# Edge router: GpSimd waits for four indirect fetches before it issues the next four

## The reference, cut to what matters

```python
h = (x_flat @ W_gat).reshape(M, HEADS, NUM_EXPERTS)          # 4 heads, 4 experts
e = leaky_relu(a_src[src] + a_dst[dst], 0.2)                 # per edge and head
ee = exp(e - e_max[dst])
denom = segment_sum(ee, dst)
msg = h[src] * (ee / denom[dst])[:, :, None]
agg = segment_sum(msg, dst) + b_gat
scores = layernorm(agg).mean over heads                      # gates the experts: top 2, softmax
```

## Time and profile before

| what | value |
|---|---|
| median of 3 timed executions | 3129.7 us (3127.84 to 3139.87) |
| span of the profiled execution | 3331.1 us |
| mean granted TensorE clock in it | 0.841 |
| edge router's loop, first fetch to the next stage's first DVE instruction | 2147.66 to 2442.31 us |
| busy shares of the span | PE 76%, DVE 63%, ACT 39%, POOL 22% |

### The profile page before, as it was taken

How to read it: one execution, slowest core, us unless ns; L and a number is a source line. 1 busy time by engine, 2 the same in 40 slices (tenths; PEclk the granted TensorE clock), 3 DMA queues, 4 the chain that set the end, 5 groups by cost and what they waited for, 6 DMA issues and landing times. The chain is left out here.

```text
span 3331.1 us, 50319 instructions
## 1 busy us (share of the span) xinstructions
PE 2524.9 (76%) x18840; PEld 1620.7 (49%) x18840; DVE 2094.1 (63%) x4114; ACT 1309.8 (39%) x2407; POOL 721.2 (22%) x756
## 2 busy tenths in 40 slices
PE   6477999999999999965566178587649989971542
PEld 5334555555555555545255167344326666641542
DVE  6737787778788878856646397654743547761212
ACT  4333444444444444424555004232224444451431
POOL 0000000000000000010064630166610033306244
PEclk7688999999999999987689557698879978885766
DMA  4431112222221121113223101000012221111333
GB/s 76 130 107 42 49 49 49 55 60 53 50 49 49 49 49 49 46 40 121 67 77 75 43 17 18 13 5 5 5 32 70 52 50 41 41 33 56 94 87 93
DMA packets 189058, 178.78 MB, mean 54 GB/s; under 512 B 83700, under 2 KB 162177, under 8 KB 185977
## 3 DMA queue, kind: packets, MB, share of 16 engines
q1 hardware_dynamic: 168064, 137.00, 16.5%
q0 software_dynamic: 20768, 38.75, 4.8%
HBM read 139.11 MB, written 43.64 MB: 55 GB/s over the span
## 5 line engine op out<-in xcount | busy, mean ns | idle before, releaser
L3557 PE MATMUL hy_ps<-hy_uT,hy_win 128*128 128x512 f32 x1152 | 499.3, 594 | 0.0
L3557 PEld LDWEIGHTS hy_ps<-hy_uT,hy_win 128*128 128x128 f32 x1152 | 217.9, 190 | 283.0 <-issue 272.2
L2469 POOL DMA_DIRECT2D ek_w<-ek_src x32 | 17.8, 556 | 1162.6 <-DVE ek_dst L2491 1162.6
L3619 PE MATMUL hy_ps<-hy_wo,hy_yg 128*128 128x512 f32 x512 | 239.6, 613 | 14.5 <-ACT XNP L3762 8.7
L3055 PE MATMUL er_c<-XNG 128*128 128x400 f32 x480 | 184.0, 540 | 0.0
L3619 PEld LDWEIGHTS hy_ps<-hy_wo,hy_yg 128*128 128x128 f32 x512 | 94.2, 193 | 125.6 <-issue 99.3
L2690 PE MATMUL f_px<-XNG 128*128 128x40 bf16 x736 | 69.0, 266 | 98.2 <-DVE XNG L2605 66.0
L3841 DVE TENSOR_TENSOR_SCAN XNG<-XNG,hy_fx 128x2048 f32<-128x2048 f32 x32 | 141.6, 4425 | 3.0 <-issue 0.4
L2988 POOL DMA_INDIRECT er_gone<-er_nodes,er_sidx x120 | 123.7, 1031 | 36.6 <-issue 36.3
L3055 PEld LDWEIGHTS er_c<-XNG 128*128 128x128 f32 x480 | 97.6, 209 | 69.5 <-issue 14.5
L946 DVE TENSOR_TENSOR f_hg<-f_hs,f_gb 128x640 f32<-128x640 f32 x64 | 52.7, 825 | 109.9 <-ACT f_hs L928 91.3
(11 more groups left out here) (698 smaller groups left out, 6123.4 us busy)
## 6 DMA issues: line engine op xcount, KB each, us to landing
XNG<-hy_decays SPq DMA_DIRECT2D x32, 1024.0 KB
hy_rb<-hy_inverse SPq DMA_DIRECT2D x128, 128.0 KB, 3.5
f_gb<-gate_rows SPq DMA_DIRECT2D x16, 640.0 KB, 5.1
g_KB<-g_keys SPq DMA_DIRECT2D x32, 320.0 KB
f_xg<-f_rows SPq DMA_DIRECT2D x54, 128.0 KB
f_ys<-f_ysl SPq DMA_DIRECT2D x54, 128.0 KB
f_y<-f_ysl SPq DMA_DIRECT2D x47, 128.0 KB
f_rows<-in_x_dram POOLq DMA_DIRECT2D x2, 2560.0 KB, 16.0
```

The source lines that it names most:

```text
L3557: mm = pe.matmul(p[:], win[:, t, m * 128:(m + 1) * 128], uT[:, t, :], start=(t == 0), stop=(t == KT - 1))
L3619: mm = pe.matmul(PS[4 + q % 2][:], yg[:, t, q * 128:(q + 1) * 128], wo[:, t, :], start=(t == 0), stop=(t == KT - 1))
```

## The change

In front of the first and of the fifth fetch of `sources`, and in front of `ends`, POOL waits for four semaphores. The values are such that the last four fetches issued have landed. A `sem_inc` on `settled`, which nobody waits for, stands behind each set of waits, as one already did behind the waits for `weighted` and `sought`. Buffers, fetches and their order stay the same.

```diff
-                def sources(par):
+                def sources(par, before):
                     for u in range(GRP):
+                        if u % PARTS == 0:
+                            for i in range(PARTS):
+                                pool.wait_ge(rows_in[par][i], before + (16 if u == 0 else 32))
+                            pool.sem_inc(settled, 1)
                         pool.indirect_dma_start(out=gone[:, par, u, :], out_offset=None, in_=tab_dram,
...
                     pool.wait_ge(weighted, r + 1)
                     pool.wait_ge(sought, r + 2)
                     pool.sem_inc(settled, 1)
+                    for i in range(PARTS):
+                        pool.wait_ge(rows_in[par][i], 24 * (r - par) + 48)
+                    pool.sem_inc(settled, 1)
                     ends(1 - par)
-                    sources(1 - par)
+                    sources(1 - par, 24 * (r + par))
...
                 ends(0)
-                sources(0)
+                sources(0, 0)
```

## The result

The changed kernel takes 3207.4 us (median of 4 executions, 3202.4 to 3218.3); the kernel before took 3134.8 us beside it on the same chip (median of 4). The ratio is **1.0256, 95% interval 1.0222 to 1.0291**: 2.6% slower, some 80 us (0.0256 x 3130). One execution of the unchanged kernel, beside `lagged` and `one_wait`, took 5077.1 us and is in no ratio. The prediction was 3188 us, with 3140 to 3222.

What follows compares the result with a forecast made beforehand. POOL's fetch issue was taken to bound the router; 36 sets at 2.0 us plus the last turns gave +75 us, or +42 with 33 regained. The middle, +58 on 3129.7, gave 3188 us, range 3140 to 3222.

Steps and rivals of the forecast that it cites:

- The bound: Fixed loop of the router: POOL issues a fetch every 1.26 us and bounds 32.1 of a pass's 37.7 us.
- A set costs 2.0 us: At each set on POOL: landing 1.56 plus restart 0.81 less the ordinary gap 0.30, taken as 2.0 us, bounds 1.2 to 2.6.
- the estimate from it: Set of waits priced by the skill page's fixed cost: 1.55 us each, sum +24 to +57, 3170 us in the middle.
- How many sets lie on the path: Sets up to turn 11's first fetches: 2 + 33 + 1 = 36, so 72 us if POOL has no idle time.
- What can be given back: POOL's pauses let PE's count through, so its idle time before `sought` vanishes: 33.4 us back, leaving +42 us.
- the six idle stretches: POOL waiting some 5.9 us for `sought` before every second turn, 1 to 11; 33.4 us in all beyond ordinary gaps.
- the middle between +42 and +75: +58 us, between all profiled idle time being in timed executions (+42) and none (+75); 3188 us, chance 0.60 for 3168 to 3208.
- The last turns: Turns 11, 12 and 13: sets partly covered by DVE's search and PE's end, adding 0.2, 1.9 and 1.4 us.
- The signs announced: New trace: 2.3 us pauses between fours, 44 us passes, `sought` waits gone to turn 11, router end about 2484 us.
- Stretches that stay with the waits on top: Rival: POOL's idle time before `sought` remains and the sets add to it; +64, 3193 us, chance 0.10.
- Dear waits of 2.6 us each: Rival: each set on POOL costs 2.6 us and no idle time is regained; +101, 3231 us, chance 0.10.
- Cheap waits and faster: Rivals: sets at 1.2 us, 3140 us, or no effect, 3130 us, together 0.12; at 0.4 us, 3111 us, chance 0.08.

Runs made afterwards that it cites:

- lagged: The kernel before plus three sets a turn, each one wait for the four fetches before the last four; 3120.7 us, ratio 0.9981.
- one_wait: The changed kernel with one wait in each set instead of four, for the last of the four fetches; 3205.3 us, ratio 1.026 to the kernel before.
- half_sources: The kernel before with only four of the eight source fetches a turn, the other rows zero; 3091.9 us, ratio 0.9893.
- the two gathers: The kernel before with five or six of eight targets gathered by TensorE, not four, so 11 or 10 fetches a turn; ratios 0.9958 and 0.9906.
- again: The kernel before, without an edit, profiled once more; 3123.0 us, ratio 1.0001, profile span 3116.7 us.
- late_sets: The kernel before with the change's sets of waits in the last two turns alone, six sets; 3143.0 us, ratio 1.0037.

## Why the prediction was right in kind and some 20 us low

**The bound: right.** POOL's fetches set the turn. `half_sources` and the two gathers show it: a fetch less makes a turn 1.1 to 1.4 us shorter, until about 12 us.

**A set costs 2.0 us: right.** The pause was expected at 2.1 to 2.5 us and is 2.17 to 2.44 up to turn 10, less 0.30 about 2.0. That it comes from asking for a fetch that hasn't landed is shown from two sides: wait for fetches that have landed and keep the sets, nothing is lost (`lagged`); take three of four waits away and keep the last fetch, nearly all stays (`one_wait`). The two parts of the sum, 1.56 us to the landing and 0.81 us to the restart, are some 1.45 and 0.9 us by the medians of the changed kernel; no run has one without the other. The Trainium skill's rule to issue a DMA early and to wait for it late ("DMA: Bandwidth & Descriptors", section "Rules for kernel authors") agrees with both runs. Its fixed cost of about 2.0 us in "Anatomy of one DMA" is below what these fetches show, 2.2 us at the least and 2.4 in the median, and the estimate from it, 3170 us, was further off.

**How many sets lie on the path: right.** The 36 sets up to turn 11's fetches were put at 72 us; between the two traces they are 69.7 us (group starts at 265.4 and 195.7 us after the first fetch). That POOL already waited 2.21 us for `sought` in one of these turns of `again` accounts for 1.9 us of the difference.

**What can be given back: wrong, and this is the step that failed.** Under "What can be given back" the six idle stretches of 33.4 us were said to vanish, and the forecast went to the middle between +42 and +75. They did vanish, but in the kernel before five of them vanish as well, and the sixth shrinks to 2.21 us (`again`). They belonged to one profiled execution, whose span was 201 us above the timed median. Next to nothing was regained, and the end of the range worked out for this case, +75, was the right one; measured were 78.9 us in the traces and some 80 in the times. The middle of +42 and +75 is 17 us below that end for this reason alone, most of the 21 us that the forecast of +58 lacks. The result stayed inside the range because the range had kept both ends. The doubt was in the text; the weight given to it was too small. The page had the warning in its first line: a profile whose span is 6% above the timed runs shows idle time that the timed runs need not have.

**The last turns: a size was off, and one mechanism.** Turns 11, 12 and 13 were put at 0.2 + 1.9 + 1.4 = 3.5 us and measured 1.5 + 2.8 + 4.9 = 9.2. One reason is the pauses of 2.9 to 3.3 us there. The other is in the term of turn 13, 4.0 - 2.6, where PE was taken to set the end. It doesn't. The ends of three traces, first the kernel before once more, where PE's last matmuls end at 2339.99:

```profile
2338.48 1.51 PE L3079 MATMUL er_c<-er_rest,er_zero 128*128 128x400 f32 x4
2344.12 0.32 DVE L3106 TENSOR_TENSOR er_W<-er_TS,er_TD 128x160 f32<-128x160 f32 x1 [15.61 <-PEq L2875]
```

then the changed kernel, where they end at 2406.29:

```profile
2404.78 1.51 PE L3086 MATMUL er_c<-er_rest,er_zero 128*128 128x400 f32 x4
2417.58 0.33 DVE L3113 TENSOR_TENSOR er_W<-er_TS,er_TD 128x160 f32<-128x160 f32 x1 [22.77 <-PEq L2875]
```

and `late_sets`:

```profile
2341.04 1.51 PE L3087 MATMUL er_c<-er_rest,er_zero 128*128 128x400 f32 x4
2355.80 0.33 DVE L3114 TENSOR_TENSOR er_W<-er_TS,er_TD 128x160 f32<-128x160 f32 x1 [24.73 <-PEq L2875]
```

From PE's end to the next stage it is 4.1, 11.3 and 13.2 us. From the start of POOL's last fetch (2334.04, 2407.59, 2345.82) it is 10.1, 10.0 and 10.0 us, and in the profile before it was 10.1 as well (2432.22 to 2442.31). Over all twelve traces it is 9.2 to 10.8 us from POOL's last fetch, and anything from 0.3 to 18.5 us from PE's end. So in the traces shown the fetches of the unused 15th group set the end of the router, and not PE, which the rows name as the releaser; no run left that group out to test it. Of the 10 us, 3.2 to 3.3 are the landing of that last fetch; what the 6.7 to 6.8 us behind it consist of was not tried.

**The signs announced.** A pass of 44 us, pauses of 2.3 us, fetches still of 0.95 us, no wait for `sought` up to turn 11, DVE's waits for the fetches in every turn: all in the trace. DVE's waits in front of `spread` are small ones of at most 1.6 us, but 30.4 us together, where "a few us" had been announced; `again` has 21.2. The router's end at 2484 us rested on the first profile and has no counterpart; against `again` it moved by 78.9 us where +75 had been worked out.

**The rivals.** Stretches that stay with the waits on top, 3193 us: no such stretch is in the changed trace. Dear waits of 2.6 us each, 3231 us: the price of the sets is wrong, but its premise, nothing to regain, was right. Cheap waits and faster: all pauses are 2.17 us or longer, and the router grew.

## What to carry to other kernels

Price a wait for one's own DMA by the rest of its landing and the restart behind it, both from the timeline, count how often it stands on the engine that sets the pace, and multiply; where the same wait is moved one group later it costs nothing. Before an idle time of the profile enters the sum, hold the profile's span against the timed median: where they are 6% apart, profile once more, or give the end without this idle time most of the weight. Where an engine is the bound by the number of its DMA issues, look for an engine that can make some of them unneeded.

## What the runs showed of the hardware that was not expected

- The late count of PE. In the first profile PE's semaphore seemed to reach DVE and ACT up to 11 us late while POOL issued fetches; in none of the eleven other profiles did DVE wait longer than 2.1 us in front of a `spread` product. That execution was longer ahead of the router and behind it as well, by 183 us together. What caused it stays open.
- 128 partitions that fetch one and the same row wait 0.8 us longer for it, 16 bytes (L2997, median 3.3 against 2.5 us to the landing) as well as 80 (L2992, 3.2 against 2.4).
- How much is in flight hardly matters: behind two fetches POOL pauses 2.0 to 2.3 us, behind four 2.2 to 2.4 (up to turn 10).
- Behind a wait for fetches that haven't landed, some 0.9 us pass from the landing to the next fetch (worked out from the medians of the changed kernel), against 0.30 us between two fetches without a pause; with one wait instead of four it is some 0.1 us less.
- A fetch takes up to 1.86 us in place of 0.95 (`again`) if it starts while DVE builds the wide one-hot pattern (L2909, 1.22 us). It then ends 0.82 to 0.84 us after L2909 has ended, in all 14 cases of `again` and in all 15 of the first profile. The first fetch behind a wait for `sought` takes 1.7 us because it falls on L2909, which DVE runs right behind `sought`; the same happens in the middle of a group, where nothing is waited for, as here in `again`. No run moves L2909 away, so the cause is read from the traces alone.

```profile
2188.08 1.22 DVE L2909 TENSOR_TENSOR er_OB<-er_spelled,er_near 128x2048 bf16<-128x2048 bf16 x1
2188.27 1.85 POOL L2988 DMA_INDIRECT er_gone<-er_nodes,er_sidx  x1 [0.30 <-issue]
```
